# Three evacuations of a graph network's pair loop, moved from ScalarE and GpSimd to VectorE

## The reference

```python
x = _layernorm(x + _L0_gnn_ref(x, edge_index, ...))   # two SAGE layers: mean over in-edges
x = _layernorm(x + _L1_gnn_ref(x, edge_index))        # degree-normalised sum
x = _layernorm(x + _L2_gnn_ref(x, edge_index, edge_weight, edge_weight_n2, ...))
x = _layernorm(x + _L3_gnn_ref(x, edge_index, edge_attr_16, ...))   # attention over in-edges
```

```python
agg = jax.ops.segment_sum(x[src], dst, num_segments=N)
mean = agg / jnp.maximum(deg, 1.0)[:, None]
h = relu(mean @ W1n + b1n + x @ W1r + x @ Wl1 + bl1)
# next: h @ W2n, which is aggregated over the edges, and h @ W2r + h @ Wl2, which is added to x
```

## Time and profile before

| | |
|---|---|
| time, median of 3 runs | 3588.99 us (3587.67 to 3591.77) |
| the profiled execution | 3591.77 us, its span 3590.0 us |
| busy, share of the span | TensorE 81%, VectorE 81%, ScalarE 62%, GpSimd 44% |
| 200 to 600 us | TensorE 378.57 of 400 us, VectorE 398.76, ScalarE 186.79, GpSimd 87.52 |
| 600 to 1000 us | TensorE 379.24 of 400 us, VectorE 398.68, ScalarE 190.88, GpSimd 89.29 |
| 1600 to 2500 us | TensorE 725.19 of 900 us, VectorE 705.53, ScalarE 693.51, GpSimd 669.99 |
| 2500 to 3590 us | TensorE 859.36 of 1090 us, VectorE 948.89, ScalarE 919.72, GpSimd 671.46 |

### The profile page before, as it was taken

One profiled execution on the slowest core, in us unless ns is written; L12 is line 12 of the kernel. 1 busy time (PEld: TensorE's weight loads), 2 busy tenths in 40 slices (PEclk: granted clock), 3 DMA queues, 4 the chain that ended last, 5 costly groups with the idle time before them and its releaser, 6 DMA issues.

```text
span 3590.0 us, 122167 instructions
## 1 busy us (share of the span) xinstructions
PE 2911.7 (81%) x50473; PEld 2637.4 (73%) x50473; DVE 2904.2 (81%) x4610; ACT 2219.8 (62%) x6003; POOL 1584.4 (44%) x1253
## 2 busy tenths in 40 slices
PE   0199999999999699899688888787768888888886
PEld 0178888888888599899677777777757777777775
DVE  7599999999999522233688888898857999999997
ACT  6334444444444400001698888898857898899887
POOL 2012222222221000000399988898964655666564
PEclk9999999999999899999899999999977888888887
DMA  8157777777777799898687877787738888888884
GB/s 221 66 157 244 237 232 234 243 237 231 234 243 236 253 370 360 330 328 320 215 279 259 264 264 248 254 271 250 257 124 302 279 278 277 276 290 274 267 278 129
DMA packets 606666, 907.43 MB, mean 253 GB/s; under 512 B 358505, under 2 KB 494858, under 8 KB 587163
## 3 DMA queue, kind: packets, MB, share of 16 engines
q1 hardware_dynamic: 583992, 800.62, 68.1%
q10 hardware_dynamic: 19763, 94.38, 7.1%
q0 software_dynamic: 2352, 4.52, 0.3%
HBM read 651.96 MB, written 247.40 MB: 251 GB/s over the span
## 4 chain that ended last, share of the span: by engine, by line
PE 36%; DVE 27%; ACT 14%; issue 10%; POOL 6%; DMA 5%; ACTq 1%; SPq 0%; DVEq 0%; POOLq 0%
PE ps L683 9%; PE ps L1047 8%; PE ps L709 4%; DMA U<-AD 4%; ACT U L1627 3%; POOL EDG L1268 3%; DVE EDG L1755 3%; DVE U L1817 3%; PE ps L696 3%; ACT U L569 3%; POOL EDG L1260 2%; ACT U L1329 2%; PE ps L667 2%; PE ps L1289 1%; DVE A L1389 1%
## 5 line engine op out<-in xcount | busy, mean ns | idle before, releaser
L569 ACT ACTIVATE U<-ps 128x512 bf16<-128x512 f32 (+1 forms) x637 | 356.4, 573 | 499.5 <-PE ps L696 475.5
L1627 ACT ACTIVATE U<-U,T 128x65 f32<-128x65 f32 x1806 | 460.1, 343 | 47.7 <-PE ps L1688 42.3
L1260 POOL TENSOR_TENSOR EDG<-U,edge 128x512 f32<-128x512 f32 (+1 forms) x196 | 214.3, 1098 | 584.1 <-DVE edge L1412 551.1
L1047 PE MATMUL ps<-U 128*128 128x192 bf16 x4802 | 418.5, 248 | 33.2 <-DMA U<-AD 32.8
L1047 PEld LDWEIGHTS ps<-U 128*128 128x128 bf16 x4802 | 402.8, 98 | 42.5 <-DMA U<-AD 39.2
L1655 POOL TENSOR_TENSOR U<-U 128x455 f32<-128x455 f32 x258 | 296.4, 1152 | 215.3 <-DVE U L1817 215.3
L866 DVE TENSOR_TENSOR EDG<-edge,EDG 128x1792 bf16<-128x1792 bf16 x343 | 367.5, 1083 | 14.4 <-DMA OSD<-EDG 12.0
L502 POOL DMA_INDIRECT U<-REC,nod x49 | 94.0, 1918 | 622.4 <-PE ps L638 501.2
L683 PE MATMUL ps<-U 128*128 128x98 bf16 (+1 forms) x5292 | 363.5, 223 | 4.5 <-DVE U L854 3.5
L709 PE MATMUL ps<-EDG,U 128*128 128x193 bf16 x2401 | 311.4, 249 | 51.1 <-ACT U L569 39.9
L683 PEld LDWEIGHTS ps<-U 128*128 128x128 bf16 x5292 | 341.3, 98 | 15.7 <-DVE U L854 11.9
(11 more groups left out here) (323 smaller groups left out, 7019.4 us busy)
## 6 DMA issues: line engine op xcount, KB each, us to landing
U<-ROWS SPq DMA_DIRECT2D x411, 448.0 KB, 4.7
U<-AD SPq DMA_DIRECT2D x98, 1568.0 KB, 8.6
OND<-EDG SPq DMA_DIRECT2D x343, 224.0 KB, 2.8
OSD<-EDG SPq DMA_DIRECT2D x343, 224.0 KB, 3.6
AD<-U ACTq DMA_DIRECT2D x49, 1568.0 KB, 5.6
EDG<-ROWS SPq DMA_DIRECT2D x171, 448.0 KB, 6.3
U<-OND SPq DMA_DIRECT2D x303, 224.0 KB, 5.9
U<-OSD SPq DMA_DIRECT2D x213, 224.0 KB, 4.7
```

The source lines that it names most:

```text
L569: ev4.by(act.activation(prow[i % NPW][:, P * g:P * (g + m)], ps[4 + gg % 2][:, 0:P * m], ACT.Copy))
L1047: ins = pe.matmul(ps[q][:, 0:192], arow[r][:, P * j:P * j + P], (XsB if p else XsA)[:, j, :, :].rearrange("p s f -> p (s f)"), start=(j == ...
L1260: ins = pool.tensor_tensor(VD[:, v:v + w, 0, KA * D:G * D].rearrange("p w (k f) -> p w k f", f=D), W_, bc(c_.unsqueeze(3), [P, w, G - KA, ...
L1627: ins = act.activation(V4[k % NV][:, 0, c, :], H[k % NHR][:, c, :], ACT.Copy, scale=a4[d % 2][:, s:s + 1])
```

## The change

Three pieces of work change engine. The slot evacuation of line 594 leaves ScalarE and becomes `slots` on VectorE, at position 1 behind `fields` and ahead of the second `hots`. The scaled copy into `cat` (line 534) becomes a VectorE instruction at position 3. The product in `ps[7]` was copied by ScalarE into a buffer `xadd` and added to X by GpSimd; now VectorE adds it to X straight from PSUM, at position 11, behind the last `hots` of the step. GpSimd keeps the addition of the bias row.

```diff
--- before.py
+++ after.py
@@ -467,7 +467,6 @@
         hid, relu, outp, t_out, x_in = sem("hidden"), sem("relu"), sem("layer_out"), sem("t_out"), sem("x_in")
         row_t, row_ev = sem("rows_t"), sem("rows_ev")
         x_ok = on(spl_a, 2)
-        xadd = [part(o2 + 6272 + D * i, D) for i in range(2)]
         over_in, over_t, bounds_t = sem("over_in"), sem("over_t"), sem("bounds_t")
         root_in, root_out = sem("root_in"), sem("root_out")
         ad_st = [sem(f"ad_st{i}") for i in range(NPW)]
@@ -489,8 +488,6 @@
 
         def pairs_pool(pool):
             def biased(i):
-                pool.wait_ge(t_out.at, i + 1)
-                x_in.by(pool.tensor_tensor(X[:, i, :], X[:, i, :], xadd[i % 2], ALU.add))
                 pool.wait_ge(x_in.at, i + 1)
                 x_ok.by(pool.tensor_tensor(X[:, i, :], X[:, i, :], brow[:, 0, :], ALU.add))
 
@@ -530,8 +527,6 @@
                     if i >= 2:
                         act.wait_ge(cat_t.at, i - 1)
                     cat_x.by(act.activation(cat[q][:, D:P], X[:, i, :], ACT.Copy))
-                    act.wait_ge(summed.at, i + 1)
-                    cat_d.by(act.activation(cat[q][:, 0:D], A[:, i, 0:D], ACT.Copy, scale=rdeg[:, i:i + 1]))
                 elif n == 5:
                     act.wait_ge(cat_t.at, i + 1)
                     if i >= 2:
@@ -544,10 +539,7 @@
                     relu.by(act.activation(hT[:, q, :], ps[7][:, P:2 * P], ACT.Relu, bias=bias1s[:, :]))
                 elif n == 9:
                     act.wait_ge(outp.at, i + 1)
-                    act.activation(T[:, i, 0:D], ps[7][:, 2 * P:2 * P + D], ACT.Copy)
-                    if i >= 2:
-                        act.wait_ge(x_in.at, i - 1)
-                    t_out.by(act.activation(xadd[q], ps[7][:, 2 * P + D:3 * P], ACT.Copy))
+                    t_out.by(act.activation(T[:, i, 0:D], ps[7][:, 2 * P:2 * P + D], ACT.Copy))
                 elif n == 11:
                     act.wait_ge(row_t.at, i + 1)
                     if i >= 2:
@@ -588,11 +580,7 @@
                 if i is not None:
                     count(i, 0)
                 if e is not None:
-                    act.wait_ge(slot_mm.at, 2 * e + 2)
-                    if e >= 2:
-                        act.wait_ge(hot8.at, NH7 * (e - 1))
-                    slot_ev.by(act.activation(sdb[e % 2].rearrange("p b s c -> p s b c"),
-                                              bc(ps[3][:, 0:2 * NB].unsqueeze(2), [P, 2 * NB, 2]), ACT.Identity, bias=sc[:, 41:42]))
+                    act.wait_ge(slot_ev.at, e + 1)
                     act.activation(E3[:, e, 0:2, :].rearrange("p f j -> p (f j)"), ps[3][:, 0:2 * NB], ACT.Identity, bias=sc[:, 41:42])
                     slot_ea.by(act.activation(E3[:, e, 2:4, :].rearrange("p f j -> p (f j)"), ps[3][:, 2 * NB:4 * NB], ACT.Copy))
                 if d is not None:
@@ -725,7 +713,7 @@
                     outp.by(pe.matmul(ps[7][:, 2 * P:3 * P], hT[:, q, :], W2c, start=True, stop=True))
                 elif n == 2:
                     if i:
-                        pe.wait_ge(t_out.at, i)
+                        pe.wait_ge(x_in.at, i)
                     pe.wait_ge(slot_ea.at, i + 1)
                     pe.transpose(ps[7][0:NB, 0:P], E3v[:, i, :, 0], ident[:, :])
                     row_t.by(pe.transpose(ps[7][0:NB, P:2 * P], E3v[:, i, :, 1], ident[:, :]))
@@ -855,6 +843,13 @@
                                         bc(l_.unsqueeze(2), [P, 8 * n, NB, 2]), ALU.mult)
                 (fld_hot if c1 == HC else dv).by(ins)
 
+            def slots(e):
+                dve.wait_ge(slot_mm.at, 2 * e + 2)
+                if e >= 2:
+                    dve.wait_ge(hot8.at, NH7 * (e - 1))
+                slot_ev.by(dve.tensor_scalar(sdb[e % 2].rearrange("p b s c -> p s b c"),
+                                             bc(ps[3][:, 0:2 * NB].unsqueeze(2), [P, 2 * NB, 2]), -1.0, None, ALU.add))
+
             def hots(i, b):
                 k = NH7 * i + b
                 r = k % NHB
@@ -873,9 +868,17 @@
                     dve.wait_ge(agg.at, i + 1)
                     dv.by(dve.tensor_reduce(A[:, i, 0:D], ps[6][:, 0:3 * D].rearrange("p (s f) -> p f s", f=D), AX, ALU.add))
                     dv.by(dve.tensor_copy(deg[:, i:i + 1], ps[6][:, 3 * D:XW]))
-                    dv.by(dve.tensor_scalar(nod[:, 1, i:i + 1], ps[6][:, 3 * D:XW], 1.0, None, ALU.max))
+                    summed.by(dve.tensor_scalar(nod[:, 1, i:i + 1], ps[6][:, 3 * D:XW], 1.0, None, ALU.max))
+                    dve.wait_ge(summed.at, i + 1)
+                    dv.by(dve.reciprocal(rdeg[:, i:i + 1], nod[:, 1, i:i + 1]))
+                elif n == 3:
+                    if i >= 2:
+                        dve.wait_ge(cat_t.at, i - 1)
                     own()
-                    summed.by(dve.reciprocal(rdeg[:, i:i + 1], nod[:, 1, i:i + 1]))
+                    cat_d.by(dve.tensor_scalar(cat[q][:, 0:D], A[:, i, 0:D], rdeg[:, i:i + 1], None, ALU.mult))
+                elif n == 11:
+                    dve.wait_ge(t_out.at, i + 1)
+                    x_in.by(dve.tensor_tensor(X[:, i, :], X[:, i, :], ps[7][:, 2 * P + D:3 * P], ALU.add))
 
             for t in range(LAST):
                 j, jb, e, i, d = at_step(t)
@@ -894,10 +897,14 @@
                             fields(jb, (1, 6).index(n), 0, 5)
                         elif n in (3, 8):
                             fields(jb, (3, 8).index(n), 5, HC)
-                    if d is not None:
+                    if e is not None and n == 1:
+                        slots(e)
+                    if d is not None and n < 11:
                         dense(d, n)
                     if i is not None and (n % 2 or n == 0):
                         hots(i, (n + 1) // 2)
+                    if d is not None and n == 11:
+                        dense(d, n)
             dve.wait_ge(x_ok.at, x_ok.o + NB)
             own()
             dv.by(dve.tensor_reduce(sc[:, 39:40], RK.rearrange("p j c k -> p (j c k)"), AX, ALU.max))
```

## The result

The changed kernel takes 3622.41 us (median, 3620.26 to 3625.03) where the kernel before takes 3590.38 (3587.67 to 3593.03): ratio 1.0091, 95% interval 1.0075 to 1.0107, 32 us slower. The forecast was 3612.5 us, which is 23.5 us slower, with a range of 3602 to 3625. The two profiled executions took 3591.77 and 3621.94 us; their spans, 3590.0 and 3620.1, are 30.1 us apart.

A forecast was written before the change was run, and what follows sets the result against it. VectorE's list was taken to bound the pair loop. 0.52 us a step gave 24.5 us, less 0.5 for step 49 and 0.5 for the tail: +23.5 us, forecast 3612.5 us, range 3602 to 3625 for 8 in 10.

The forecast's parts named there:

- The bound: Pair loop's steady part: VectorE busy 947.93 of 951.00 us; every 0.1 us added to its list is added to the step.
- The slot evacuation: Line 594 moved to VectorE, steps 2 to 49: costs 0.27 us a step, bounds 0.17 to 0.35.
- The addition to X: Line 550 and GpSimd's line 493 moved to VectorE, steps 4 to 49: 0.13 us a step, bounds 0.10 and 0.22.
- The scaled copy: Line 534 moved to VectorE, steps 4 to 49: 0.12 us a step, bounds 0.09 and 0.22.
- GpSimd's disturbance: GpSimd adds slowing VectorE in the loop: 0.08 us a step, kept as it is; bounds -4 and +2 us.
- the case given 8%: GpSimd's remaining add holds VectorE its full 0.32 us in each of 46 steps: 11 us higher, 3623.5; 8% within the forecast.
- The waits: Waits of the moved VectorE instructions cost nothing in the loop; ScalarE's copies to E3 are covered by 1.1 us.
- The tail: Behind 1190.63 us moved work is spare; a shorter last link and ScalarE's shorter queue give together -0.5 us.
- The rival of a faster kernel: The ring of TensorE and ScalarE is the bound; line 594 gone saves 14 us, 3575; chance 4%.
- its ring: Loop's ring of TensorE and ScalarE, nearly as long as VectorE's, with only about 0.2 us of slack a step.
- The rival of a new wait: In the loop, exposed waits and late E3 copies make it much slower: 51 us, 3640; chance 6%.

The follow-up runs named there:

- E3: Not a run: a buffer in the pair loop that ScalarE's copies write (line 596); no kernel or measured time goes by this name.
- the ScalarE experiment: Kernel before with the bfloat16 slot evacuation (line 594) left out from block 2 on: 3590.76 us against 3593.61 beside it, ratio 0.999.

## Why the prediction was right, and where it was off

**The bound** was read rightly: VectorE's list. Every experiment that shortened it shortened the step, and relieving ScalarE gave 0.02 us. The 3 us of 951 in which VectorE is idle in the kernel before stand ahead of lines 832 and 878, where it waits for its own last result. The whole came out 8.5 us slower than forecast (32 instead of 23.5), inside the range but near its upper end. Most of that lies in terms that were mis-sized, as follows.

**The slot evacuation**, 0.27 us forecast: 0.27 measured. **The addition to X**, 0.13: 0.13 to 0.14. **The scaled copy**, 0.12: 0.16 to 0.17, within its bounds. Its row lasts 0.24 us where 0.18 to 0.21 were forecast. The neighbour it was read from the earlier trace rows has 49 elements and constants; this one has 64 elements and a scale that is read from memory, one per partition, and no run separates the two. 46 x 0.045 = 2 us.

**GpSimd's disturbance** was the largest mis-sized term, and it went beyond its own bound. Forecast: 0.08 us a step kept as it is, +2 us at most. Measured: 0.12 us in every step at line 820 and 0.06 beside GpSimd's transfer, 0.18 against 0.08, some 5 us over the loop. The first was within what the prediction allowed for the addition; that the record transfer would come to start together with a VectorE instruction was not thought of. In the case given 8%, the addition would have cost the whole 0.32 us a step, more than twice the 0.12 that it did.

**The loop's opening** was not costed apart: step 4 opens 1.8 us late (221.75 against 219.98). Of these, 0.8 are there when step 2 opens, ahead of any changed instruction; 0.5 are the two slot evacuations of steps 2 and 3, which the forecast has. The rest, 0.5 us, is a new wait in step 2, where the pieces of later steps give no cover. ScalarE's copies to E3 wait for VectorE, and VectorE's rank reductions then wait for TensorE:

```profile
191.77 0.34 ACT L584 ACTIVATE E<-ps,sc 128x98 f32<-128x98 f32 x1 [1.33 <-DVE EDG L850]
```

```profile
199.93 1.14 DVE L825 TENSOR_REDUCE EDG<-ps 128x10 bf16<-128x490 f32 x2 [0.38 <-PE ps L655]
```

The second wait is absent in the kernel before and with the slot evacuation back on ScalarE, and present with either other part undone. Added up, 23.5 + 2 + 5 + 0.5 = 31 us. That stands between the two measures, 30.1 us by the spans and 32.0 by the medians, and each of these moves by some us from one execution to the next.

**The waits** forecast as covered were covered in the steady part: VectorE shows none before the three new rows, and ScalarE none for line 850 from step 4 on. The step was forecast at 21.6 to 21.7 us and is 21.80, and the loop ends 30.8 us later, not 24.

**The tail** gained about what was said at its last link: lines 550, 493 and 495 have become one addition of 0.22 us and 492, and from ScalarE's last copy to T to VectorE's next instruction it is 0.91 us (1261.07 to 1261.98) instead of 1.16 (1230.04 to 1231.20), where 0.3 less was forecast.

**The rival of a faster kernel** fell with the ScalarE experiment, and the length of its ring (20.97 us) confirms the 0.2 us of slack read from TensorE's waits. The rival of a new wait, at 6%, fell too: its 51 us did not come, and the one new wait that delays VectorE in steps 2 to 47 stands in step 2.

## What to carry to other kernels

Where an engine's rows follow one another without idle time, price a moved instruction by the interval to the next row, and multiply; what the other engines gain is worth nothing until that list gets shorter, even where the chain of waits runs through them. Two rings can be within 1% of each other: leave out work on either side to learn the other's length. Before moving instructions off a full engine, look for a wait on its own last result and put another instruction in between.

## What the runs showed of the hardware

The order in which GpSimd and VectorE start decides who pays, and a few tenths of a microsecond turn it round. When GpSimd's record transfer began together with a 3136-element bfloat16 VectorE instruction (two operands in SBUF), it took 0.92 us and the instruction 1.82 or 1.83 instead of 1.77: 41 of 42 transfers in the changed kernel. When it began 0.13, 0.25 or 0.27 us later (the addition moved to position 9, the addition undone, the slot evacuation undone), it took 2.3 to 2.45 us and VectorE lost nothing. In the kernel before, GpSimd's addition cost VectorE 0.12 to 0.13 us in all 28 steps in which it got in first, and nothing in the 16 in which it was held. A GpSimd addition of 0.31 us cost VectorE 0.12 us ahead of a 1764-element bfloat16 instruction, and nothing under reductions from PSUM.

"SBUF — State Buffer" in the Trainium skill, section "SBUF: two separate sides", has the one that starts first keep the shared ports for its whole instruction while the other is blocked. Where GpSimd was the later one, the traces agree: it was held until behind the end of VectorE's instruction (614.68 + 2.30 = 616.98, VectorE's ended at 616.18). Where GpSimd started first or at the same instant, they do not fit VectorE as blocked for the whole of it: it lost 0.06 us to a transfer of 0.92 and 0.12 to an addition of 0.31.
